# A new instruction order for the second stage of a windowed-attention network on one core

## The reference

```python
for i in range(DEPTH):                                   # DEPTH = 6
    x = attn_layer(shift_tokens(x), Wqkv[i], q_scale[i], k_scale[i], Wo[i]) + x
    x = ffn_layer(shift_tokens(x), ln_g[i], ln_b[i], W1[i], b1[i], W2[i], b2[i]) + x
# attn_layer: q, k l2-normalised and rotated, 16 heads of 64, each window of 32 tokens sees
# itself and the window before; softmax(8 * q k); times v; times Wo
# ffn_layer: layernorm, W1 (128 -> 2 x 341), a * gelu(gate), W2
```

## Time and profile before

| what | value |
|---|---|
| runs of the kernel (3) | 4816.96, 4825.4, 4829.28 us; median 4825.4 |
| profiled execution | 4821.14 us, span 4819.4 us |
| PE busy over the span | 4087.5 us (85%) |
| DVE / ACT / POOL busy | 3990.3 (83%) / 2994.8 (62%) / 3489.3 (72%) |
| 40 slices, PE, last 25 | 9 tenths or more |
| granted clock of PE in slices 16 to 39 | 9 tenths or more |

### The profile page before, as it was taken

How to read it: one execution, slowest core, us unless ns; L and a number is a source line. 1 busy time by engine, 2 the same in 40 slices (tenths; PEclk the granted TensorE clock), 3 DMA queues, 4 the chain that set the end, 5 groups by cost and what they waited for, 6 DMA issues and landing times.

```text
span 4819.4 us, 153868 instructions
## 1 busy us (share of the span) xinstructions
PE 4087.5 (85%) x60260; PEld 2123.1 (44%) x60260; DVE 3990.3 (83%) x7132; ACT 2994.8 (62%) x4240; POOL 3489.3 (72%) x1655
## 2 busy tenths in 40 slices
PE   3666666666655999999999999999999999999997
PEld 1222333223322455555555555555555555555554
DVE  6999999999973788888888888888888888888884
ACT  5999999999982455545554555555555455554552
POOL 4999899999984666667666676666666676666762
PEclk9755555555556999999999999999999999999998
DMA  0000000000003445544445444454454444454443
GB/s 14 3 6 5 10 5 9 5 10 5 3 7 81 101 105 118 118 113 102 111 113 123 109 107 111 118 122 103 103 118 119 113 102 110 118 127 101 107 111 102
DMA packets 230497, 381.82 MB, mean 79 GB/s; under 512 B 38112, under 2 KB 59232, under 8 KB 229728
## 3 DMA queue, kind: packets, MB, share of 16 engines
q1 hardware_dynamic: 229856, 372.57, 32.9%
HBM read 51.57 MB, written 18.61 MB: 15 GB/s over the span
## 4 chain that ended last, share of the span: by engine, by line
PE 47%; issue 5%; DVE 5%; POOL 4%; SPq 3%; DMA 3%; ACT 2%; DVEq 0%; POOLq 0%
PE pb L1396 11%; PE pb L1454 7%; PE pb L1414 6%; PE pb L1437 6%; PE pb L1401 5%; PE pb L1465 3%; PE pb L1448 3%; SPq L1230 3%; PE pb L1477 3%; POOL sqs L1822 3%; DMA qkn<-nf 3%; ACT sq L1674 2%; DVE nf L1957 2%; PE pb L1424 1%; DVE m L1934 1%
## 5 line engine op out<-in xcount | busy, mean ns | idle before, releaser
L734 POOL TENSOR_TENSOR W<-W 128x1280 f32<-128x1280 f32 x416 | 955.5, 2321 | 141.3 <-ACT W L585 139.8
L1822 POOL TENSOR_TENSOR sqs<-sq 128x1024 f32<-128x1024 f32 x192 | 469.3, 2444 | 763.6 <-ACT sq L1674 763.6
L585 ACT ACTIVATE W<-S,lam 128x512 f32<-128x512 f32 (+3 forms) x2048 | 952.3, 554 | 84.0 <-DVE lam L878 72.6
L1826 POOL TENSOR_TENSOR m<-m 128x1024 f32<-128x1024 f32 x384 | 947.3, 2483 | 18.9 <-DVE m L1934 17.4
L849 DVE BATCH_NORM_STATS2 stats<-W 128x6 f32<-128x512 f32 (+3 forms) x2048 | 832.5, 479 | 57.6 <-POOL W L734 56.5
L1396 PE MATMUL pb<-xs,wg 128*128 128x512 f32 x1536 | 733.9, 606 | 14.9 <-DMA xs<-hist 14.5
L1933 DVE TENSOR_TENSOR m<-pb,tab 128x1024 f32<-128x1024 f32 x384 | 467.0, 1216 | 132.9 <-ACT sq L1674 119.9
L1674 ACT ACTIVATE sq<-pb 128x1024 f32<-128x1024 f32 x384 | 393.4, 1025 | 280.0 <-PE pb L1396 279.5
L1957 DVE SCALAR_TENSOR_TENSOR nf<-rn,m 128x1024 f32<-128x1024 f32 x384 | 513.9, 1358 | 53.7 <-POOL m L1826 46.4
L1679 ACT ACTIVATE lnn<-pb,cst 128x1024 f32<-128x1024 f32 x192 | 212.6, 1107 | 496.2 <-PE pb L1401 496.1
L1837 POOL TENSOR_TENSOR pr<-pr,rsum 128x1024 f32<-128x1024 f32 x192 | 365.5, 1904 | 181.1 <-DVE rsum L1970 181.1
(11 more groups left out here) (123 smaller groups left out, 7380.8 us busy)
## 6 DMA issues: line engine op xcount, KB each, us to landing
qkn<-nf SPq DMA_DIRECT2D x1536, 128.0 KB, 2.4
vr<-v SPq DMA_DIRECT2D x96, 768.0 KB, 5.9
vr<-v SPq DMA_DIRECT2D x96, 192.0 KB, 5.5
xr<-hist SPq DMA_DIRECT2D x48, 256.0 KB, 4.8
hist<-xo SPq DMA_DIRECT2D x47, 256.0 KB, 4.9
wg<-wqkv SPq DMA_DIRECT2D x24, 384.0 KB, 3.4
xs<-hist SPq DMA_DIRECT2D x48, 128.0 KB
vr<-v SPq DMA_DIRECT2D x96, 64.0 KB, 6.4
```

The lines of the kernel that those rows point to most:

```text
L585: ins = nc.scalar.activation(W[:, p, h, c], S[:, j % 2, h, c], ACT.Abs_reciprocal_sqrt, bias=lam[:, j, i:i + 1])
L734: nc.gpsimd.tensor_tensor(W[:, p, h, :], W[:, p, h, :], W[:, p, h, :], ALU.mult).then_inc(s_wp[p], 1)
L1822: nc.gpsimd.tensor_tensor(sqs[:, :, :], sq[:, :, 0, :], sq[:, :, 1, :], ALU.add).then_inc(s_sqs, 1)
L1826: nc.gpsimd.tensor_tensor(m1[:, which, :, :], m1[:, which, :, :], m2[:, which, ::-1, :], ALU.add)\
```

## The change

No instruction is added to or taken from the elementwise engines, and no product changes. Moved are steps in all five orders, and banks:

- PE: `mean` goes from the third place of the body (item b-2) to its end (item b-1, the same item, two steps earlier in time). `up1` now stands before `score2`. The waits of `q0` stand before `score2` and its products after it. The waits of `v0` stand directly before its products. `weigh2`'s second half stands before `score0`'s first. The waits of `v2` stand before `score1`'s first half, then `v2`, then `norm2` with its waits.
- Banks: `out` 4 (was 5), `mean` 4 (4), `wo` 5 (2), `v2` 2 (4); the rest as before.
- ACT: `exponentials` 1 before `log_norms` 3. `squares` (2,1) before (2,0), both before `exponentials` 0. `values` 2 before `log_norms` 2.
- POOL: `square_sums` 2 before `less_max` 0; `normalise` 0 before `add_rotated` (2,1), both now written at the head of the next body.
- DVE: `denominators` 1 before `weighted` 0; `finish` (3,0) before `mask` 2 and `finish` (3,1) after it; `row_max` 0 after `weighted` 3; `centre` before `mask` 1; `finish` (2,1) before (2,0); `inverse_denominators` 2 between the two `finish` of group 0.
- SP: `rolled(b, 0)` becomes `rolled(b-1, 0)` at the head of the next body; `load_xr`, `load_w1` and the loads of groups 2 and 3 stand earlier.

The diff, cut to what is spoken of below:

```diff
         HOLD = [
-            ("k3", 1, 6), ("mean", 2, 4), ("q3", 1, 0), ("var", 2, 2), ("v3", 1, 4), ("turn0", 1, 2),
-            ("norm3", 1, 6), ("weigh0", 1, 4), ("gate0", 2, 2), ("gate1", 2, 6), ("score2", 1, 4), ("up1", 2, 7),
...
-            ("weigh2", 1, 6), ("norm1", 0, 4), ("score0", 0, 2), ("out", 2, 5), ("turn3", 1, 6), ("q2", 0, 0),
-            ("weigh3", 1, 2), ("k2", 0, 6), ("wo", 1, 2), ("score1", 0, 0), ("norm2", 0, 6), ("v2", 0, 4),
+            ("k3", 1, 6), ("q3", 1, 0), ("var", 2, 2), ("v3", 1, 4), ("turn0", 1, 2), ("norm3", 1, 6),
+            ("weigh0", 1, 4), ("gate0", 2, 2), ("gate1", 2, 6), ("up1", 2, 7), ("score2", 1, 4), ("q0", 0, 0),
...
+            ("norm1", 0, 4), ("score0", 0, 2), ("out", 2, 4), ("turn3", 1, 6), ("q2", 0, 0), ("weigh3", 1, 2),
+            ("k2", 0, 6), ("wo", 1, 5), ("score1", 0, 0), ("v2", 0, 2), ("norm2", 0, 6), ("mean", 1, 4),
         ]
@@ PE body @@
-                if live(b, 2):
-                    take("mean", b)
-                    residual_due(b - 2)
-                    mean(b - 2, bank("mean"))
...
                     take("up1", b)
+                    ups(b - 2, 1, bank("up1"))
+                if live(b, 0):
+                    take("q0", b)
+                    weights_due(b, 0)
+                    inputs_due(b)
                 if live(b, 1):
                     take("score2", b)
                     rotated_due(b - 1, 2)
                     scores(b - 1, 2, 0, bank("score2"))
                 if live(b, 1):
                     scores(b - 1, 2, 1, bank("score2"))
-                if live(b, 2):
-                    ups(b - 2, 1, bank("up1"))
...
                     norms(b, 1, bank("norm1"))
+                if live(b, 1):
+                    weigh(b - 1, 2, 1, bank("weigh2"))
                 if live(b, 0):
                     take("score0", b)
...
+                if live(b, 1):
+                    take("mean", b)
+                    residual_due(b - 1)
+                    mean(b - 1, bank("mean"))
@@ ACT body @@
                     turned(b, 0)
                 if live(b, 0):
+                    exponentials(b, 1)
+                if live(b, 0):
                     log_norms(b, 3)
                 if live(b, 0):
                     inverse_norms(b, 3)
-                if live(b, 0):
-                    exponentials(b, 1)
@@ POOL body @@
+                if live(b, 1):
+                    normalise(b - 1, 0)
+                if live(b, 1):
+                    add_rotated(b - 1, 2, 1)
...
+                    square_sums(b, 2)
+                if live(b, 0):
                     less_max(b, 0)
                 if live(b, 0):
-                    square_sums(b, 2)
-                if live(b, 0):
-                    add_rotated(b, 2, 1)
@@ DVE body @@
                     finish(b, 0, 0)
+                if live(b, 1):
+                    inverse_denominators(b - 1, 2)
                 if live(b, 0):
                     finish(b, 0, 1)
-                if live(b, 1):
-                    inverse_denominators(b - 1, 2)
...
                     rotate(b, 3, 0)
                 if live(b, 0):
+                    denominators(b, 1)
+                if live(b, 0):
                     weighted(b, 0)
                 if live(b, 0):
-                    denominators(b, 1)
-                if live(b, 0):
                     inverse_denominators(b, 1)
                 if live(b, 0):
+                    finish(b, 3, 0)
+                if live(b, 0):
                     mask(b, 2)
                 if live(b, 0):
                     finish(b, 3, 1)
-                if live(b, 0):
-                    finish(b, 3, 0)
                 if live(b, 1):
                     gate(b - 1, 2)
```

More of the change, by code:

```diff
@@ L1273, in body @@
                 if live(b, 1):
+                    rolled(b - 1, 0)
+                if live(b, 1):
                     rotated(b - 1, 2)
@@ L1279, in body @@
                 if live(b, 1):
+                    load_xr(b - 1)
+                if live(b, 1):
+                    load_wo(b - 1, l, k == 1)
+                if live(b, 0):
+                    load_projections(b, l, k == 0, (2, 3))
+                if live(b, 1):
                     rotated(b - 1, 3)
@@ L1283, in body @@
                 if live(b, 1):
-                    load_wo(b - 1, l, k == 1)
-                if live(b, 0):
-                    load_projections(b, l, k == 0, (2, 3))
+                    load_w1(b - 1, l, k == 1)
                 if live(b, 1):
@@ L1292, in body @@
                     load_vectors(b - 1, l, k == 1)
-                if live(b, 0):
-                    rolled(b, 0)
-                if live(b, 0):
-                    load_xr(b)
                 if live(b, 2) and not is_body(b, END + 2):
                     store(b - 2)
-                if live(b, 1):
-                    load_w1(b - 1, l, k == 1)
             for b in range(BATCH):
@@ L1547, in body @@
                     scores(b - 1, 2, 1, bank("score2"))
-                if live(b, 2):
-                    ups(b - 2, 1, bank("up1"))
                 if live(b, 0):
-                    take("q0", b)
-                    weights_due(b, 0)
-                    inputs_due(b)
                     project(b, 0, 0, bank("q0"))
@@ L1557, in body @@
                     project(b, 0, 1, bank("k0"))
-                if live(b, 0):
-                    take("v0", b)
-                    weights_due(b, 1)
                 if live(b, 1):
@@ L1565, in body @@
                 if live(b, 0):
+                    take("v0", b)
+                    weights_due(b, 1)
                     values(b, 0, bank("v0"))
@@ L1611, in body @@
                     scores(b, 0, 0, bank("score0"))
-                if live(b, 1):
-                    weigh(b - 1, 2, 1, bank("weigh2"))
                 if live(b, 2):
@@ L1642, in body @@
                 if live(b, 0):
-                    take("norm2", b)
-                    squares_due(b, 2)
+                    take("v2", b)
+                    weights_due(b, 3)
                 if live(b, 0):
@@ L1649, in body @@
                 if live(b, 0):
+                    values(b, 2, bank("v2"))
+                if live(b, 0):
+                    take("norm2", b)
+                    squares_due(b, 2)
                     norms(b, 2, bank("norm2"))
[L1651 to L1654, removed]
+                if live(b, 1):
+                    take("mean", b)
+                    residual_due(b - 1)
+                    mean(b - 1, bank("mean"))
             pe.wait_ge(const_in, 80)
@@ L1771, in body @@
                 if live(b, 0):
+                    squares(b, 2, 1)
+                if live(b, 0):
                     squares(b, 2, 0)
@@ L1775, in body @@
                 if live(b, 0):
-                    squares(b, 2, 1)
+                    values(b, 2)
                 if live(b, 0):
@@ L1780, in body @@
                     inverse_norms(b, 2)
-                if live(b, 0):
-                    values(b, 2)
                 if live(b, 0):
@@ L1882, in body @@
                 if live(b, 0):
+                    square_sums(b, 2)
+                if live(b, 0):
                     less_max(b, 0)
                 if live(b, 0):
-                    square_sums(b, 2)
-                if live(b, 0):
-                    add_rotated(b, 2, 1)
-                if live(b, 0):
                     add_rotated(b, 2, 0)
-                if live(b, 0):
-                    normalise(b, 0)
             for t in (xm[:, :], xs[:, :], qkn[:, :, :, :, :]):
@@ L2066, in body @@
                 if live(b, 0):
-                    row_max(b, 0)
-                if live(b, 0):
                     finish(b, 1, 0)
@@ L2071, in body @@
                     weighted(b - 1, 3)
+                if live(b, 0):
+                    row_max(b, 0)
                 if live(b, 0):
@@ L2083, in body @@
                     residual(b - 1)
+                if live(b, 1):
+                    centre(b - 1)
                 if live(b, 0):
@@ L2086, in body @@
                 if live(b, 0):
+                    finish(b, 2, 1)
+                if live(b, 0):
                     finish(b, 2, 0)
[L2088 to L2091, removed]
                 if live(b, 0):
@@ L2104, in body @@
                 if live(b, 0):
+                    denominators(b, 1)
+                if live(b, 0):
                     weighted(b, 0)
                 if live(b, 0):
-                    denominators(b, 1)
+                    inverse_denominators(b, 1)
                 if live(b, 0):
-                    inverse_denominators(b, 1)
+                    finish(b, 3, 0)
                 if live(b, 0):
```

## The result

The changed kernel takes 4863.0 us (median of 4 runs, 4861.8 to 4871.17) against 4821.18 (4 runs, 4815.18 to 4829.28) for the kernel before: 1.0092 of its time, 95% interval 1.0079 to 1.0104. The forecast was 4866 from a median of 4825.4, a ratio of 1.0084. The profiled execution took 4863.57 us, with a span of 4861.8.

What follows compares the result with a forecast made beforehand. PE's products were taken to set stage 2's pace. Per body +1.15 + 0.2 - 0.45 = +0.9 us, over 46 bodies +41 us, so a median of 4866 us; range 4800 to 4890.

Steps and rivals of the forecast that it cites:

- The collision (steps 2, 4 to 6): In group 3, DVE's finish (3,0) waits for all of POOL's normalise 1; mask 2 follows late, gate ends 1.15 us late.
- DVE first: Rival: finish (3,0) gets the port before normalise 1; -0.3 us per body, 4811 us; chance 0.18.
- No collision: Rival: normalise 1 comes later or times shift by over a us; -0.95 us per body, 4782 us; chance 0.10.
- a lost second meeting: Rival: POOL's normalise 2 takes the port before DVE's finish (0,1); +2.0 us per body, 4917 us; chance 0.12.
- Who waits (step 7): On PE, k0 waits for mask 2 and turn1 for gate; the two coincide, shift at turn1 +1.15 us.
- step 1: Head of the body: var may start some 0.2 us late, covered by PE's 0.25 wait at norm3; cost 0.
- The DMAs (step 8): score3 waits for SP's 8 DMAs of nf group 3, 8.24 us after finish; that stays, so +1.15 us there too.
- a sign: On PE, turn1 to score3 should have its old length, 7.3 us.
- The second meeting: Mid-body, DVE's finish (0,1) goes before POOL's normalise 2, which waits up to 1.2 us; turn2 0.2 us late.
- The second half: weigh2's second half covers PE's wait for rotate at score0: gain 0.41 us, bounds 0.2 to 0.6.
- The small gains of waits ahead of small products: On PE, the waits of q0 and v2 now stand ahead of small products: 0 to 0.1 us gained each.
- the ends: Stage 1 and the ends of stage 2 give nothing either way.

Runs made afterwards that it cites:

- Kernels 1 to 3: Changed kernel with inverse_denominators 1 behind finish (3,0), 4830.51 us; changed kernel with POOL's two group 3 add_rotated swapped, 4814.07 us; and kernel 3.
- Kernel 4: The kernel before with only weigh2's second half moved ahead of score0: 4819.69 us, 0.9987 of before.
- kernel 5: The kernel before with weigh2's second half ahead of score0 and gated_due's waits ahead of take(out): 4802.26 us, 0.9967 of before.
- kernel 3: The kernel before with only finish (3,0) moved ahead of mask 2: 4873.32 us, 1.010 of before.
- kernel 6: The kernel before with only gated_due's waits moved ahead of take(out), weigh2 left in place: 4819.02 us, 1.0005 of before.

## Why the prediction was right, and where it was not

*The collision (steps 2, 4 to 6)* was right in place, mechanism and size. Forecast for `finish` (3,0): 2.9 us over `normalise`; measured 2.91. Kernels 1 to 3 show it as the cause: avoiding it in two different ways brings the time back to within 0.2% of before, and the one move that makes it brings the whole loss to the kernel before. The rival "DVE first" hung on which instruction starts first; it was POOL, by 0.07 us. "No collision" and a lost second meeting did not come either: both meetings are in the timelines above.

*Who waits (step 7)* was right: `k0` for `mask` 2, 1.34 us. `gate` ends 17.78 us after `var`, before 16.81 (2720.14 - 2703.33): +0.97, where 1.15 was forecast. Most of the rest is step 1: `var` itself starts some 0.2 late, as estimated there, and the distances are counted from it (`norm3` comes 3.74 us after `var`, before 3.91).

*The DMAs (step 8)* were right in that the delay is handed on, and off in size: "the 8.24 stay" did not hold. `score3` starts 8.50 us after `finish` (3,1) ends (2742.10 - 2733.60), and `turn1` to `score3` is 7.55 instead of its old 7.28, which was named as a sign. The shift there is +1.23, near the forecast's +1.15 only because 0.97 and another 0.26 add up to it. Why the way through the DMAs grew was not looked into.

*The second meeting* was right in who goes first (DVE, by 0.16), and wrong in its cost: `normalise` 2 took 0.85 longer, but `turn2` did not come later. 0.2 was put in, 0 was found.

*The second half* was the term that failed, the largest one behind the collision. "PE waited 0.41 for `rotate` (1,1) at `score0`. ... Gain 0.41": nothing was gained, `norm1` to `out` is 4.56 us before and after. I counted the 0.28 before `out` as issue time that stays at 0.28, because the profile names no releaser there. `out` also waits for `log_norms` 1, through the bank it shares with `norm1`, and then goes through four more waits. That chain has its own length (in both kernels `out` starts 0.75 us after `log_norms` 1 ends) and ran just behind the wait that I took away. Kernel 4 shows that the wait only moves, kernel 5 that the chain is what holds it. The small gains of waits ahead of small products were not tried by themselves; in the sum none is to be seen.

*The sum.* Forecast per body +0.9 (+1.15, +0.2, -0.45). Found in this body: +1.17, that is +1.23 up to `score3` and next to nothing behind it. The total came out near because of a second term that the forecast put at nothing: the ends. The `var` step of the kernel before, then of the changed one (windows 1600 to 4750 us and 1600 to 4800; 94 records are 47 of the 48 steps; shortest, median and longest in ns; first and last start in us):

```profile
L1461 PE MATMUL pb<-xc,avg x94: 591/593/649, 1617.5 to 4724.9; 128*128 128x512 f32 x94
```

```profile
L1461 PE MATMUL pb<-xc,avg x94: 592/667/682, 1612.7 to 4772.8; 128*128 128x512 f32 x94
```

The same from 4700 to 4850 us, which holds the 48th step, again before and after:

```profile
L1461 PE MATMUL pb<-xc,avg x4: 591/592/667, 4724.5 to 4784.8; 128*128 128x512 f32 x4
```

```profile
L1461 PE MATMUL pb<-xc,avg x6: 592/675/1190, 4704.1 to 4828.2; 128*128 128x512 f32 x6
```

Between the first and the 47th lie 3107.4 and 3160.1 us: +52.7, or +1.15 a body over 46. The first `var` comes 4.8 us earlier, and the time behind the 47th is 89.0 instead of 94.5; most of these 5.5 us lie between the 47th and the 48th (55.4 instead of 59.9). Together 42.4, the difference of the two spans. So two misses, +0.25 per body (11 us) and -10 at the ends, cancel. That the total of 4863 came so near to 4866 is luck; the collision, forecast at 2.9 us and found at 2.91, is not. Where the ends' 10 us come from was not settled: the first `var` came between 1609 and 1616 us in the other kernels, those made from the kernel before among them, and kernel 3, whose only edit is the one `finish`, also has a short end.

## What to carry to other kernels

Before a DVE instruction with two SBUF inputs is made to wait for a POOL result, look at what POOL has next: if that is ready, DVE may come second by a hair (here 0.07 us) and wait for all of it; order DVE's own step that readies it behind, or let DVE's input come one POOL instruction earlier, so that it stands waiting when the port comes free. Before a wait is taken away, look for the next one that ends within its length behind it, in releasers that the profile names only once they come last. In a chain of waits ahead of an instruction put the one that ends last at the end; it pays only where nothing else ends at the same time (kernel 5 against kernel 6).

## What the runs showed of the hardware

A DVE `finish` and a POOL instruction excluded each other by who was standing first, in both directions, and to within 0.07 us: 2.91 for a `finish` that came 0.07 behind `normalise` instead of 1.2, 2.75 for a `normalise` 0.16 behind `finish` instead of 1.9, and 2.88 where POOL's next was recorded 0.02 before the end of the instruction that DVE stood waiting for, but DVE had stood there for 1.4 us. The time that the loser stands there is inside its own record, as busy time, and not shown as idle time. Waits that are already met are not free when they stand behind a late one: four of them, each with the raising of a semaphore behind it, made PE start 0.75 us after the releaser's end instead of 0.47.
